# Loading x1 tile by tile in the combining pass, instead of into one large tile during the expert tiles

## The reference

```python
x = x + layernorm(attn(layernorm(x)))    # RWKV time mixing: xk, xv, xr -> k, v, r; wkv scan; Wo
x = x + layernorm(ffn(layernorm(x)))
# ffn: 8 experts of inner size 256, the best 2 of each token, and a shared expert of 512
scores = softmax(xt @ gate_w.T + gate_b);  top_w, top_i = top_k(scores, 2)
expert_e = (silu(xt @ w1.T + b1) * (xt @ w3.T + b3)) @ w2.T + b2
y = sum over e of gate[t, e] * expert_e;  z = shared expert
return y + z
```

## Time and profile before

| | us |
|---|---|
| timed runs, median (lowest to highest) | 1258.77 (1258.77 to 1259.7) |
| profiled execution | 1250.62 |
| its span, first to last instruction | 1248.8 |
| PE busy in the span | 1012.4 |
| DVE busy | 892.7 |
| POOL busy | 844.3 |
| ACT busy | 508.4 |

### The profile page before, as it was taken

The page is one execution under the profiler, slowest core; times in us unless marked ns, Lnnn a source line. Parts: engine busy times, 40 slices in busy tenths (PEclk is TensorE's granted clock), DMA queues, the critical chain, the costliest instruction groups (busy, mean ns, idle before and its releaser), DMA issues. The chain is left out here.

```text
span 1248.8 us, 23009 instructions
## 1 busy us (share of the span) xinstructions
PE 1012.4 (81%) x6344; PEld 892.5 (71%) x6344; DVE 892.7 (71%) x2147; ACT 508.4 (41%) x885; POOL 844.3 (68%) x1047
## 2 busy tenths in 40 slices
PE   0557789889988998899889676778999999988553
PEld 0446578777777777687778566777999999988432
DVE  4677898779878877978797523456777667566496
ACT  3223433453445344534453233333444434333175
POOL 2244887887798779878887753145776667565498
PEclk9777999999999999999999779798999999899755
DMA  4232232443244224414532226579878898898586
GB/s 130 61 106 89 93 97 82 149 140 92 88 147 139 82 90 156 128 57 127 155 106 66 83 74 216 172 182 231 145 145 180 181 224 167 189 229 199 106 251 221
DMA packets 114548, 174.05 MB, mean 139 GB/s; under 512 B 13485, under 2 KB 93768, under 8 KB 112200
## 3 DMA queue, kind: packets, MB, share of 16 engines
q1 hardware_dynamic: 83304, 121.09, 32.5%
q0 software_dynamic: 26592, 35.67, 15.8%
q10 hardware_dynamic: 4608, 16.78, 3.6%
HBM read 173.53 MB, written 78.21 MB: 202 GB/s over the span
## 5 line engine op out<-in xcount | busy, mean ns | idle before, releaser
L1477 POOL DMA_INDIRECT sum_y<-e_y,e_row_at x142 | 222.7, 1569 | 42.9 <-issue 36.7
L1311 PE MATMUL e_h_ps<-e_z_hi,e_w 128*128 128x256 f32 x1136 | 223.5, 291 | 27.3 <-DMA e_w<-w_split 13.2
L1311 PEld LDWEIGHTS e_h_ps<-e_z_hi,e_w 128*128 128x128 f32 x1136 | 187.6, 198 | 29.7 <-issue 17.7
L1132 POOL DMA_INDIRECT slots_x<-f_xf,f_at x128 | 145.5, 1137 | 32.4 <-issue 32.1
L1311 PE MATMUL e_h_ps<-e_z_lo,e_w 128*128 128x256 f32 x568 | 163.9, 289 | 0.0
L1353 ACT ACTIVATE e_act_h<-e_h_ps,e_w 128x256 f32<-128x256 f32 x142 | 67.4, 475 | 201.9 <-PE e_h_ps L1311 201.9
L618 PE MATMUL f_h_ps<-f_f_hi,f_w_hi 128*128 128x512 f32 x256 | 109.1, 426 | 29.7 <-DVE f_h L900 25.8
L1327 PE MATMUL e_y_ps<-e_w,e_h_hi 128*128 128x256 f32 x568 | 118.4, 292 | 1.1 <-DVE e_h_lo L1399 1.1
L1392 DVE SCALAR_TENSOR_TENSOR e_h<-e_h_ps,e_w,e_act_h 128x256 f32<-128x256 f32 x142 | 68.1, 483 | 71.1 <-ACT e_act_h L1353 70.4
L1311 PEld LDWEIGHTS e_h_ps<-e_z_lo,e_w 128*128 128x128 f32 x568 | 112.1, 197 | 0.0
L862 DVE RECIPROCAL f_den<-f_den 128x256 f32<-128x256 f32 (+1 forms) x48 | 109.6, 2283 | 1.1
(11 more groups left out here) (227 smaller groups left out, 3038.9 us busy)
## 6 DMA issues: line engine op xcount, KB each, us to landing
e_w<-w_split SPq DMA_DIRECT2D x71, 1026.0 KB
e_w<-w_split ACTq DMA_DIRECT2D x71, 512.0 KB
e_x_in<-slots_x SPq DMA_DIRECT2D x71, 260.0 KB, 2.8
f_x_in<-x SPq DMA_DIRECT2D x16, 512.0 KB, 5.2
f_x_res<-x SPq DMA_DIRECT2D x16, 512.0 KB, 6.2
x_dram<-f_x SPq DMA_DIRECT2D x16, 512.0 KB, 7.0
sum_y<-f_y SPq DMA_DIRECT2D x32, 256.0 KB, 2.2
c_x<-x_dram SPq DMA_DIRECT2D x32, 256.0 KB
```

What stands on the lines that cost most here:

```text
L1132: pool.indirect_dma_start(out=slots_x[:, :], out_offset=bass.IndirectOffsetOnAxis(ap=at[p][:, j, k:k + 1], axis=0), in_=xf[p][:, j, :], in ...
L1311: last = pe.matmul(h_ps[q][:, which, :], w13(p, part)[:, which, c, q * P:(q + 1) * P], z[p % 2][:, c, :], start=(n == 0), stop=(n == 5))
L1477: pool.indirect_dma_start(out=dst[:, :], out_offset=bass.IndirectOffsetOnAxis(ap=row_at[p][:, j:j + 1], axis=0), in_=y[p][:, j, :], in_off ...
```

## The change

The argument `load_x1` and its calls in the expert stage go, and with them the large tile. The combining pass gets four tile buffers for x1 and loads each tile (512 KB, all partitions) behind the load of acc. POOL's addition waits for its own tile's load instead of one wait for all loads ahead of the pass.

```diff
@@ expert_tiles, SP
-                if inside(i - LOOP[0], TOKENS // P) and par % 2 == 0:
-                    load_x1(sp, i - LOOP[0], par // 2)
                 load_x(i + 4, par)
@@ combine
-        eye, b_out, x1 = (ahead[n] for n in ("eye", "b_out", "x1"))
+        eye, b_out, b_ready = (ahead[n] for n in ("eye", "b_out", "b_ready"))
         acc = [sb(f"acc{p}", [P, SUBS, C]) for p in range(DEPTH)]
+        x1 = [sb(f"x1{p}", [P, SUBS, C]) for p in range(DEPTH)]
-        b_ready, x1_loaded = (ahead[n] for n in ("b_ready", "x1_loaded"))
+        x1_loaded = [sem(f"x1_loaded{p}") for p in range(DEPTH)]
@@ combine, SP
             for i in range(tiles):
                 wait(sp, normed, i - DEPTH + 1)
                 sp.dma_start(acc[i % DEPTH][:, :, :], rows(acc_dram, i)).then_inc(acc_loaded[i % DEPTH], 16)
+                wait(sp, res_ready, i - DEPTH + 1)
+                sp.dma_start(x1[i % DEPTH][:, :, :], rows(x1_dram, i)).then_inc(x1_loaded[i % DEPTH], 16)
@@ combine, POOL
-            pool.wait_ge(x1_loaded, 16 * 2 * tiles)
@@ combine, POOL, add_x1
                 wait(pool, stored[s % DEPTH], 16 * (s // DEPTH))
+                pool.wait_ge(x1_loaded[s % DEPTH], 16 * (s // DEPTH + 1))
                 pool.tensor_tensor(res[s % DEPTH][:, :, :], normal[s % 2][:, :, :],
-                                   x1[:, s * SUBS:(s + 1) * SUBS, :], ALU.add).then_inc(res_ready, 1)
+                                   x1[s % DEPTH][:, :, :], ALU.add).then_inc(res_ready, 1)
@@ sandwich
-                 "gates": sb("c_gates", [P, NT, 3 * (E + 1)], F32R), "x1": sb("c_x1", [P, NT, C])}
...
-        expert_tiles(nc, TILES, 2, slots_x, sum_y, w_split, own_s, out_biases, tile_of, gates, ahead, load_x1)
-        combine(nc, sum_y, ahead, out.rearrange(tokens))
+        expert_tiles(nc, TILES, 2, slots_x, sum_y, w_split, own_s, out_biases, tile_of, gates, ahead)
+        combine(nc, sum_y, x1_dram.rearrange(tokens), ahead, out.rearrange(tokens))
```

More of the change, by code:

```diff
@@ L1157, in _, with expert_tiles @@
             steps(pool, body, -1, *LOOP, END)
-def expert_tiles(nc, tiles, parts, slots, dst, weights, own_s, out_biases, tile_of, gates, ahead, load_x1):
+def expert_tiles(nc, tiles, parts, slots, dst, weights, own_s, out_biases, tile_of, gates, ahead):
     C = dst.shape[1]
@@ L1488, in _, with combine @@
             steps_by_four(pool, body, 0, *LOOP, tiles + 2)
-def combine(nc, acc_dram, ahead, out):
+def combine(nc, acc_dram, x1_dram, ahead, out):
     C = acc_dram.shape[1]
@@ L1698, in sandwich @@
         ahead = {"eye": eye, "b_out": sb("c_b_out", [3 * (E + 1), C], F32R),
-                 "gates": sb("c_gates", [P, NT, 3 * (E + 1)], F32R), "x1": sb("c_x1", [P, NT, C])}
[L1700 to L1709, removed]
-        expert_tiles(nc, TILES, 2, slots_x, sum_y, w_split, own_s, out_biases, tile_of, gates, ahead, load_x1)
-        combine(nc, sum_y, ahead, out.rearrange(tokens))
+                 "gates": sb("c_gates", [P, NT, 3 * (E + 1)], F32R), "b_ready": ctx.enter_context(nc.semaphore("c_b_ready"))}
+        expert_tiles(nc, TILES, 2, slots_x, sum_y, w_split, own_s, out_biases, tile_of, gates, ahead)
+        combine(nc, sum_y, x1_dram.rearrange(tokens), ahead, out.rearrange(tokens))
 def kernel(**inputs):
```

## The result

The change made the kernel faster: 1249.95 us (median of 10 runs, 1245.28 to 1254.87) against 1257.62 us (10 runs, 1253.15 to 1265.74), a ratio of 0.9937 with a 95% interval of 0.9916 to 0.9959. Forecast were 1262.8 us, slower. Beside the experiments the changed kernel ran twice more, at 0.9961 [0.9928, 0.9994] and 0.9970 [0.9941, 0.9999]. Set against the runs of before of the same call, the mean of the changed kernel lies 7.9, 5.0 and 4.3 us lower; weighted by their errors that is 5.7 us faster, with a standard error of 0.8. Three runs of before that strayed far in a slower state (1266.52, 1268.37 and 3387.6 us) are left out of every mean here.

What follows compares the result with a forecast made beforehand. PE was taken to bound the expert stage and POOL the combining pass, DMA engines close behind; 1258.77 us plus 6.6 for added loads less 2.6 for removed ones gave 1262.8 us, range 1253 to 1269.

Steps and rivals of the forecast that it cites:

- What bounds the stages: Expert stage: PE, without gaps except where the expert changes; combining pass: POOL, 3.78 us a tile, DMA engines close behind.
- What goes, 2.6 us: Expert stage: removing x1 loads ahead of second weights at four changes of expert gives back 2.6 us.
- rival C: Expert stage: all x1 loads in saturated stretches delay PE, 7.4 us back, 6.6 lost, 1258.0 us; chance 0.12.
- What comes, 6.6 us: Combining pass: x1 loads make DMA work 4.57 us a tile against 3.78, adding 6.6 us after slack.
- The lower bound: Combining pass: all three transfers of a tile at 414 GB/s take 3.80 us, and nothing is lost.
- rival A: Combining pass: engines keep 414 GB/s beside stores, so the pass costs nothing; -2.6, 1256.2 us; chance 0.28.
- The slack: Combining pass: acc would still land 2.9 us before its use, taken off the 9.5 us of added DMA time.
- rival D: Combining pass: mixed traffic capped at 353 GB/s, 5.2 us lost, +2.6 in all, 1261.4 us; chance 0.14.
- The clock: Expert stage: a clock dropping at a new place could cost 1.5 us, used only as a bound.
- The sum: Whole kernel: +6.6 in the combining pass less 2.6 in the expert stage, +4.0 us, slower.

Runs made afterwards that it cites:

- e4: Kernel before without any x1 load, POOL adding the normalised rows to themselves; ratio 0.9915 to before, 10.9 us below it.
- e5: Kernel before without any x1 load, POOL adding a zeroed tile of its own instead; ratio 0.9946 to before, 5.9 us below it.
- e9: Kernel before with x1 loads only at changes of expert (seven loads), POOL adding a zeroed tile; ratio 0.9994 to before.
- e10: Kernel before with x1 loads only away from changes of expert (25 loads), POOL adding a zeroed tile; ratio 0.9980 to before.
- e1: Kernel before, unchanged, run again for a second profile; ratio 1.0017 to before.
- e8: Changed kernel with 8 instead of 4 buffers each for acc, x1 and res in the combining pass; ratio 0.9951 to before.

## Why the prediction was wrong

- **What bounds the stages** was right. e4 shows that POOL paces the pass, and the 25 loads away from the changes are worth little, 0.1 us each, if anything.
- **What goes, 2.6 us, was mis-sized**: the loads were worth 5.9 us (e5) or 4.2 (e4). The step that failed is the count. I took four of the changes, those with an x1 load in front of second weights that PE waited for in one execution, and only that wait; the other 28 loads I put at nothing. In fact the seven loads at changes cost 4.7 us in e9, 0.67 each, and the 25 others perhaps 2.4 (e10). This is rival C, which put 7.4 us on it. The waits that the term was built on did not shrink either: at second weights PE waited 5.07 us in all in the first profile of before and 5.55 in e1, and 5.14, 3.90 and 4.87 in the three profiles of the changed kernel. They move from change to change with each execution (e1 has 1.40, 1.29, 0.71 and 2.15 us, partly at other changes than before), so one profile of them couldn't carry a term of the sum. How a load at a change delays PE, by the first weights, the second or the scatters, stays open.
- **What comes, 6.6 us, was mis-sized**: it is 1.8 us (74.0 against 72.2). I added 1.27 us to the 3.30 us that the queues were taken for, 4.57 a tile. Of those 3.30 us, 0.75 (2.02 less 1.27) were the cold start of a load, and in a queue with two loads that share shrank: the load queue took 2.78 us a tile instead of the 3.29 forecast, both queues 4.06. The places were right: DVE waits for acc from the eighth tile on, acc lands after 7.6 us, POOL has gaps. The lower bound, 414 GB/s for everything, was the near end; rival A had it.
- **The argument against A was wrong by the trace of before.** I wrote that every streaming microsecond I could point at was loads alone, and pointed at one of both queues at 197 GB/s. From 1205 to 1206 us of the same pass the store queue moved 61 packets and the load queue 54, together 406 GB/s (packets, MB, share of 16 engines):

```profile
q10 hardware_dynamic: 61, 0.25, 60.6%
q1 hardware_dynamic: 54, 0.16, 39.2%
```

- **The slack** of 2.9 us explains why so little is left: a pace of 3.84 to 4.01 us at 410 to 392 GB/s (1,572,864 bytes) is at most 0.2 us over 3.78, for 12 tiles 2.8 us, which the slack would cover. The pass still lost 1.8 us, in waits of DVE for acc. Eight buffers take them away (e8), so they come from loads issued too late and not from the rate.
- **The ceiling of 353 GB/s** (rival D) does not exist for 4 KB packets: loads and stores together keep 414 GB/s in e8. By that the limit of 358 GB/s that the prediction cites did not bind here either. The Trainium skill's page HBM Reference, section Specifications (TRN2), says that a core streaming alone measures about 425 GB/s; the 414 of e8 lie close to that.
- **The clock** had no term. In the first pair of profiles PE's busy time in the expert stage fell by 3.8 us at a clock of 0.96 instead of 0.94, but over the seven profiles without x1 loads in the stage the busy time is 344.4 to 349.7 us, against 348.0 and 348.3 before. A help from the clock is neither shown nor excluded.
- **The sum**: -5.9 + 1.8 = -4.1 us from the parts, or -2.4 with e4's figure; measured are -5.7. The errors are 0.8 on this and 1.1 to 1.3 on the first part, so the parts may be all of it, and a further gain of up to some 3 us isn't excluded. The range, from 1253 us, assumed that A and C don't come true together. They nearly did, and the two belong to one mistake: in both stages I judged by an average share where the bytes' place in time decided. The base was high as well: the three runs of before that I had gave 1258.77 us, where the runs of before of all calls have a mean of 1255.3. That moves the forecast by 3 us and doesn't excuse its sign.

## What to carry to other kernels

Where a queue's busy share is made of single transfers that start cold, it overstates what more bytes will cost: work out both ends, bytes over the streaming rate and cold transfers, and take the streaming end if the added load goes out beside another one. A prefetch that is free on average can sit at the worst place: look what the DMA engines do in the moments when the bounding engine waits, and count every transfer issued in these, not only the one in front of a wait of the profile at hand. Before calling a rate unseen, list several windows by queue. Take several profiles before comparing stages of a kernel whose executions differ by more than the change, and trust a mechanism seen in one pair of them only when the others repeat it.

## What the runs showed of the hardware

- POOL's addition of two float32 sources of 128 x 1024 takes 2.35 us if they are different tiles and 1.89 us if both are the same tile (16 instructions each, e5 and e4).
- The same expert stage, with the same transfers and no x1 loads, took 394.5 us in one profiled execution (e4) and 386.4 in another (e5).
- Loads and stores of 4 KB packets mixed keep 414 GB/s over 50 us at a DMA share of 1.03 (e8). Before, with loads that start alone, 44 us of the pass showed a share of 0.91 and only 273 GB/s:

```profile
1190.00:1234.00 44.00, 25.05 (x88) 17.02 (x88) 42.82 (x126) 30.62 (x58) 40.91 (x37) 0.50 0.91 273
```
